# Products of an identity put among the maxima of an attention kernel, and six in front of each attention core

## The reference

```python
x = x + attention_a(layernorm(x))
x = x + experts(layernorm(x))
x = x + attention_b(layernorm(x))
x = x + experts(layernorm(x))
```

```python
scores = (q @ k.T + bias) / sqrt(16), causal
w = softmax(scores, axis=-1)
out = (w @ v) @ Wo + bo
```

## Time and profile before

| | us |
|---|---|
| median of 3 runs | 1968.99 (1961.76 to 1969.76) |
| the profiled execution, its own time | 1967.3 |
| span of the profiled execution | 1965.5 |
| PE busy (matmul) | 1680.7 |
| PE weight loads | 1039.2 |
| DVE busy | 1428.1 |
| ACT busy | 1127.5 |
| POOL busy | 695.3 |

### The profile page before, as it was taken

How to read it: one execution, slowest core, us unless ns; L and a number is a source line. 1 busy time by engine, 2 the same in 40 slices (tenths; PEclk the granted TensorE clock), 3 DMA queues, 4 the chain that set the end, 5 groups by cost and what they waited for, 6 DMA issues and landing times.

```text
span 1965.5 us, 36378 instructions
## 1 busy us (share of the span) xinstructions
PE 1680.7 (86%) x12410; PEld 1039.2 (53%) x12410; DVE 1428.1 (73%) x3057; ACT 1127.5 (57%) x1999; POOL 695.3 (35%) x788
## 2 busy tenths in 40 slices
PE   6899999999978799987788999999999777889910
PEld 5545444445556677774334454544446566777710
DVE  5678888888577865885547788888865787558843
ACT  2145767577557677764233558585674676776710
POOL 6000101000257556445660001010012674754466
PEclk9678989899979999998895789898998898999965
DMA  6540120300065656665752204031002555666643
GB/s 233 173 70 2 24 45 13 56 2 2 31 265 165 182 172 199 207 198 184 239 188 50 32 2 64 4 49 18 2 7 101 217 175 166 204 189 201 203 146 118
DMA packets 127906, 225.96 MB, mean 115 GB/s; under 512 B 15364, under 2 KB 91028, under 8 KB 123444
## 3 DMA queue, kind: packets, MB, share of 16 engines
q1 hardware_dynamic: 103152, 156.49, 26.4%
q0 software_dynamic: 24576, 67.14, 12.5%
HBM read 124.20 MB, written 98.84 MB: 113 GB/s over the span
## 4 chain that ended last, share of the span: by engine, by line
PE 57%; DVE 12%; DMA 11%; issue 7%; POOL 7%; ACT 3%; SPq 1%; ACTq 0%; DVEq 0%; POOLq 0%
PE late_banks L1721 14%; PE late_banks L1679 12%; PE exp_banks L1707 8%; PE late_banks L1510 6%; PE exp_banks L1527 6%; POOL ring_t L1086 4%; DMA ring_t<-token_rows,index_t 4%; DMA ring_t<-expert_rows,rows_of_t 3%; DVE inter_t L2020 3%; POOL ring_t L1081 2%; DVE chunk_max_t L2139 2%; DMA expert_rows<-outs_t 2%; PE late_banks L1485 2%; PE late_banks L1685 2%; PE late_banks L1543 2%
## 5 line engine op out<-in xcount | busy, mean ns | idle before, releaser
L1339 ACT ACTIVATE probs_t<-exp_banks 128x1024 f32<-128x1024 f32 (+3 forms) x640 | 539.2, 896 | 294.6 <-PE exp_banks L1707 292.0
L2139 DVE TENSOR_REDUCE chunk_max_t<-late_banks 128x1 f32<-128x512 f32 (+1 forms) x960 | 603.0, 682 | 115.8 <-PE late_banks L1679 89.6
L1177 POOL TENSOR_SCALAR_AFFINE_SELECT probs_t<-probs_t 128x512 f32<-128x512 f32 x128 | 81.2, 635 | 681.5 <-ACT probs_t L1339 681.5
L1721 PE MATMUL late_banks<-probs_t,values_t 128*32 128x512 f32 (+3 forms) x2560 | 320.0, 575 | 1.9 <-POOL probs_t L1177 1.1
L1086 POOL DMA_INDIRECT ring_t<-expert_rows,rows_of_t x256 | 243.7, 952 | 188.9 <-DVE x_sb_t L2038 126.6
L1510 PE MATMUL late_banks<-tokensT_t,fetched_t 128*128 x2048 | 297.5, 290 | 11.5 <-ACT fetched_t L1243 5.1
L1081 POOL DMA_INDIRECT ring_t<-token_rows,index_t x256 | 248.7, 972 | 140.5 <-PE late_banks L1485 83.4
L2020 DVE TENSOR_TENSOR inter_t<-late_banks,silu_t 64x256 f32<-64x256 f32 x512 | 217.5, 425 | 89.1 <-ACT silu_t L1260 78.2
L1510 PEld LDWEIGHTS late_banks<-tokensT_t,fetched_t 128*128 128x128 f32 x2048 | 254.1, 195 | 41.9 <-issue 23.0
L1679 PE MATMUL late_banks<-contextT_t,Qp_t 50*128 50x512 f32 (+7 forms) x640 | 234.4, 515 | 9.6 <-DVE chunk_max_t L2139 2.2
L1527 PE MATMUL exp_banks<-fetched_t,inter_t 64*128 64x128 f32 x2048 | 187.6, 303 | 45.8 <-DVE inter_t L2020 43.7
(11 more groups left out here) (228 smaller groups left out, 1886.4 us busy)
## 6 DMA issues: line engine op xcount, KB each, us to landing
expert_rows<-outs_t SPq DMA_DIRECT2D x256, 256.0 KB
weights_t<-in_experts SPq DMA_DIRECT2D x8, 1728.0 KB, 13.8
Qp_t<-q_rows SPq DMA_DIRECT2D x12, 768.0 KB
weights_t<-in_experts SPq DMA_DIRECT2D x4, 2112.0 KB, 10.4
q_rows<-part_hi_t SPq DMA_DIRECT2D x16, 512.0 KB, 3.9
k_rows<-part_hi_t SPq DMA_DIRECT2D x16, 512.0 KB, 4.5
Kp_t<-k_rows SPq DMA_DIRECT2D x8, 768.0 KB
q_rows<-part_lo_t SPq DMA_DIRECT2D x16, 256.0 KB, 5.1
```

The lines of the kernel that those rows point to most:

```text
L1339: act.activation(probs[:, e % NP, 2 * p:2 * p + 2, off:QB], exp_banks[sq % 2][:, :, off:QB], ACT.Exp, scale=D ** -0.5).then_inc(exp_done, 1)
L1721: last = pe.matmul(pv_banks[n % NPV][32 * h:32 * h + 32, off:QB], values[:, j, GH * g + h, :], probs[:, e % NP, h, off:QB], start=(j == 0) ...
L2139: op = dve.tensor_reduce(chunk_max[:, b, p, chunk_row(r), chunk_col(b, r, c)], bank[:, 0:n].rearrange("q (p k) -> q p k", p=len(parts)), A ...
```

## The change

Two constants are added, `FILL_RUN` and `OPENING_FILLS`, both 6. A new function `with_fills` goes over the finished plan. It gathers stretches of items without `qk`, `pv`, `turn_ctx` and `project`. In a stretch with six maxima or more it puts an item `("fill", n)` behind each maximum with an odd number, except behind the last maximum and directly ahead of a turn; `n` is the number of score products so far. PE alone knows this item: it multiplies the 16-bit identity by itself, broadcast to 512 columns, twice, into the pair of `exp_banks` that the next score product will overwrite. The first fill of each `n` waits until the exponentials of that pair are made. Besides, six such products into BANK[0] stand in front of the core, ahead of the waits for freed banks and values. Nothing reads any of these products. The results of the kernel don't change.

```diff
+FILL_RUN, OPENING_FILLS = 6, 6
...
+def with_fills(plan):
+
+    filled, run, scored = [], [], 0
+
+    def close(run):
+        maxima = [n for n, item in enumerate(run) if item[0] == "max"]
+        for n, item in enumerate(run):
+            filled.append(item)
+            second_half = item[0] == "max" and item[3] % 2 == 1
+            if len(maxima) >= FILL_RUN and second_half and n < maxima[-1] and run[n + 1][0] != "turn":
+                filled.append(("fill", scored))
+
+    for item in plan:
+        if item[0] in ("max", "turn", "ctx", "out", "scale", "divide"):
+            run.append(item)
+            continue
+        close(run)
+        run = []
+        filled.append(item)
+        scored += item[0] == "qk"
+    close(run)
+    return filled
...
 def build(nc, A, parts="afbf"):
-    plan = core_plan()
+    plan = with_fills(core_plan())
...
+                pe.wait_ge(ident_ready, 10)
+                wide = ident16[:, :, :].rearrange("p a c -> p (a c)").rearrange("p (o c) -> p o c", o=1)\
+                    .broadcast_to([P, 2, 2 * P])
+                last_unit = core_unit[layer] - 1
+                wait_freed(pe, last_unit - last_unit % NBANK)
+                for _ in range(OPENING_FILLS):
+                    pe.matmul(BANK[0].rearrange("p (o c) -> p o c", o=2), ident16[:, 0, :], wide, start=True, stop=True)
                 wait_all_freed(pe, core_unit[layer])
-                pe.wait_ge(ident_ready, 10)
                 pe.wait_ge(values_set, 2 * layer + 2)
-                begun = set()
+                begun, begun_fills = set(), set()
...
+                    elif item[0] == "fill":
+                        sq = layer * SQ + item[1]
+                        if sq >= 2 and sq not in begun_fills:
+                            pe.wait_ge(exp_done, sq - 1)
+                        begun_fills.add(sq)
+                        for half in range(2):
+                            pe.matmul(exp_banks[sq % 2][:, half, :].rearrange("p (o c) -> p o c", o=2), ident16[:, 0, :],
+                                      wide, start=True, stop=True)
```

## The result

The changed kernel takes 1981.34 us in the median of 7 runs (1978.82 to 1992.18); the kernel before, in 7 runs on the same chip, 1963.01 (1954.74 to 1969.76). The ratio is 1.0097, with an interval of 1.0074 to 1.0121: slower by 1%. The forecast of 1962 is 19 us too low, and the result lies just outside the range, past its upper end of 1980. The change run once more, later, gave 1.0077 (1.0044 to 1.0109).

A forecast was written before the change was run, and what follows sets the result against it. It took DVE to bound the runs without scores, and PE the scores behind them. Against the profiled 1967.3 us, (a) -3, (b) -5, (c) +3 and (d) 0 gave -5: 1962 us, range 1942 to 1980.

The forecast's parts named there:

- A fill at full clock: Between pairs of maxima: a fill takes PE 0.45 us; with pair and load 1.10 to 1.19, just hidden by DVE's 1.22.
- (d): Fills at diagonals, where PE has little room: 0 to +4 us, taken as 0.
- (a): Four runs with the next block's diagonal, PE-bound in small part when cold: at most 3.9 us gained, taken as -3.
- A load that can't be hidden: Weight loads of fills: priced as running beneath full-array products, as the trace shows, against the skill's rule.
- Rival B: Every pair with a fill: loads laid bare, PE bounds the runs, 0.36 us more per fill, 1989 us; chance 0.14.
- Does the clock stay?: Clock holds through the run, falls at first scores in most of twelve places after 4.6 to 5 us without dense products.
- The sum: Both cores, forecast case: the terms together -5 us against the profiled 1967.3, giving 1962 us.
- the cores' cold time falls to under 120: Sign against the forecast: time at half clock in both cores falling from 235 to under 120 us.
- (b): First scores behind runs: starting at full clock brings the first probabilities-and-values group 0.8 us earlier, half counted, twelve times: -5.
- (c): First block of each core, cold throughout, four fills each at 0.9 us: between 0 and +7 us, taken as +3.
- A: Clock holds through first scores: 1931 us in all twelve places, chance 0.10; about 1948 in part of them, chance 0.20.
- C: Fills don't move the clock at all and cost only where PE is tight: 1970 us; chance 0.08.

The follow-up runs named there:

- number 2: The changed kernel with fills only behind pairs of maxima without diagonal chunks, 13 per core in place of 42; ratio 0.9992.
- number 7: Full-row fills and bridging fills only behind 208 and 240 score products of each core, no opening products; ratio 1.0017 against the kernel before.
- number 5: The changed kernel with each fill as four products of 64 rows, two in each half of the array; ratio 0.9993 against the kernel before.
- number 9: number 6 with fills also directly ahead of turns, 48 per core instead of 42; 1937.93 us, ratio 0.9862 against the kernel before.
- number 6: number 5 plus 25 bridging fills per core up to the first probabilities-and-values group; ratio 0.9977, on a third chip 0.9933, against the kernel before.

## Why the prediction was wrong

*A fill at full clock*: **this is the step that failed.** It set 0.45 for the fill, 2 x 0.23 for the pair and 0.19 to 0.28 for a load against DVE's 1.22 us, "just hidden by DVE". The rows behind it are of full-array products among their own kind and of whole maxima. For whole pairs it holds roughly (0.16 us each in number 2). But 29 of 42 fills of a core stand at diagonals, where two maxima take PE 0.95 us only because they run beside each other, and a fill between them costs 1.01. Term (d), "fills at diagonals", said 0 to +4 and was taken as 0; it measures about 12 over the eight runs (number 2). Behind it stands the sentence "In the runs without scores PE is not the bound", read from six whole maxima; at a diagonal DVE waited 0.36 and 0.28 us for PE even before, at full clock; (a) had such idle time come from the cold clock. I read no row of a switch between products of 50 rows and of 128, though the trace has such neighbours: the group at 121.76 in the earlier trace rows stands among maxima.

*A load that can't be hidden*: half right. Between the fill's own two products the load is hidden, as the earlier trace rows said. The load behind the fill, for a maximum of 50 rows, is not: it starts 0.42 us behind the fill's load. The Trainium skill's rule, TensorE: Matmul & The Clock Gate, section "What overlaps and what doesn't", speaks of just this, a load that can't run beneath a product that uses its rows. The trace agrees with it on the switch and disagrees on the fill's own pair. Rival B took the rule for both and priced 0.36 us for all 84 fills, 30 us, 1989; measured are 14 us in the runs, most of it from the diagonals. B had the direction and what the profile would show, at about twice the size in the runs. Its chance of 0.14, and the 0.12 for slower, were too low.

*Does the clock stay?* Right that it would be up for more of the runs and down at the first scores: 58 us at half clock became 21, and 75 became 78. Wrong on where it falls. I had it hold through the run and counted 4.6 to 5 us without a dense product behind the last fill; in seven of the eight runs it fell 1.6 to 5.6 us before the run's end, with the last fill not yet done (in six of eight, 1.7 to 4.6 us, when the change ran again). So fills between the maxima didn't by themselves make the run dense enough. "The forecast is wrong if the cores' cold time falls to under 120": it is 184. "Or if the runs get longer": they do, which is what failed.

*The sum.* (a), -3 for the runs at full clock, is buried in +14.2. (b), -5, didn't come: the scores behind the eight runs are 1.9 us longer, those from 8 and from 240 add 1.8. A fall among scores, where PE is the bound, costs what one in a run does not. These few us are no more than what two executions of one kernel differ by there, but a gain of 5 is not in them. (c), +3 for the first blocks, was nearer to -3: up to the scores behind 8, the first core is 5.0 us shorter, the second 2.2 longer. That gain isn't the fills' doing, as far as the runs show. The second execution of the change doesn't have it (10.73 us for the first eight scores and 15.74 for the run behind them, where the first had 8.92 and 12.27), and number 7, with no fill or opening product there, does (8.56 and 11.71). Together: +14.2 for the runs, +1.0 for the rest of the cores, -1.2 outside.

*The rivals.* A did not come with the change, but its price was sound. It had the first group of probabilities and values 3.1 us behind the first score at full clock, and in number 5 it comes at 2.97 and 3.17 behind 48. It had 1931 us with the clock held in all twelve places, and the profiled execution of number 9 takes 1934.2; the eight places gain 2.0 to 2.7 us each (269.3 or 275.0 less 253.6). C is out: the fills move the clock (184 and 201 against 246 twice, and 31 with the thin stretch closed), and those of 64 columns do not (263).

What stays open: why six more fills per core ahead of the turns bring half clock from 78 to 31. That they do it and not chance, the runs of both on one chip show. The times are 0.9933 and 0.9862, with intervals that don't meet, so that the six are worth 0.7%, and the granted clock over the span is 0.938 to 0.945 in all six runs of number 9, 0.916 to 0.934 in the twelve of number 6 and 0.883 to 0.893 in those of the kernel before. Where they stand fits: the longest time without a fill in the second half of a run is around the turn (3.4 us behind 208 scores in the change, from 375.13 to 378.55, with the fall at 379.45), and they cut it to 2.2 us. One fall is left there, at 370.34 us of number 9, so that this gap is the reason isn't shown apart.

## What to carry to other kernels

When you put a cheap product between others, ask what ran side by side there: the price of an instruction on TensorE is what it pushes apart, and products that kept to one half of the array, as their neighbours do, cost a third of those that take all of it (0.35 against 1.01 us here). Products that are to hold the clock may have to fill the thin places inside a stretch and go on up to the next dense work. Here fills in halves alone left the time as it was (number 5, 0.9993), with the bridges it gained 0.7% (number 6, on the third chip), and with the turns filled too 1.4%. Count a gain only when it comes back in a second execution: half clock differed by 17 us between two of the same kernel. And measure the price at the tightest place (the diagonals), not at the one whose rows are easiest to read.

## What was not expected of the hardware

- A full-array fill between two maxima of 50 rows costs 0.65 us at full clock with two products of 64 columns, 0.81 with one of 512 and 1.01 with two of 512 (1.60, 1.76 and 1.96 against 0.95 us for the maxima alone). So most of it doesn't go with the columns. The same fill in products of 64 rows runs beside the maxima, 0.35 us for twice as many instructions.
- PE can read as fully busy while its granted clock is down: from 1260 to 1277 us of the changed kernel, 17.00 of 17.00 us busy at 0.50.

```profile
1260.00:1277.00 17.00, 17.00 (x72) 7.16 (x70) 10.51 (x19) 8.26 (x9) 0.00 (x0) 0.50 0.01 2
```
